# bs_w's weights loaded first and its first quarter made ahead of the one-hot rows; the last unit's gate and up products one unit further up

## What is computed

```python
# layer 0: one expert per sequence, the argmax of cond_8
expert = argmax(cond_8, -1)
up, gate = x @ W_up[expert].T + b_up, x @ W_gate[expert].T + b_gate
x = x + (silu(up) * gate) @ W_down[expert].T + b_down
# layer 1: a base matrix and a low-rank part, weighted by cond_8
x = x + x @ W_base.T + b_base + 2.0 * einsum('bter,eor,be->bto', einsum('btc,erc->bter', x, As), Bs, cond_8)
# layer 2: a weighted sum of eight masked matrices
x = x + einsum('bnt,bot->bno', x, einsum('bg,got->bot', cond_8, weight * mask)) + bias
# layer 3: the two best experts of each sequence and a shared one (gelu MLPs, 128 -> 512 -> 128)
x = x + sum over the 2 chosen of w * mlp(x, expert) + mlp(x, shared)
```

## Time and profile before

| | us |
|---|---|
| median of 3 runs | 153.5 (153.43 to 153.65) |
| the profiled execution | 153.69 |
| its span, first to last instruction | 151.7 |
| PE busy | 147.4 (97% of the span) |
| DVE, ACT, POOL busy | 109.8, 72.0, 91.4 |

### The profile page before, as it was taken

The page is one execution under the profiler, slowest core; times in us unless marked ns, Lnnn a source line. Parts: engine busy times, 40 slices in busy tenths (PEclk is TensorE's granted clock), DMA queues, the critical chain, the costliest instruction groups (busy, mean ns, idle before and its releaser), DMA issues.

```text
span 151.7 us, 3108 instructions
## 1 busy us (share of the span) xinstructions
PE 147.4 (97%) x1075; PEld 135.1 (89%) x1075; DVE 109.8 (72%) x229; ACT 72.0 (47%) x138; POOL 91.4 (60%) x93
## 2 busy tenths in 40 slices
PE   7999999999999999999999999999999999999992
PEld 2479999999978999999989999999999999999881
DVE  3985666667996586867775967876587895968772
ACT  2875444461375554454444354545425434345640
POOL 1003999999700007849994939995876999880000
PEclk9999999999999999999999999999999999999999
DMA  2999999974354676393397386095447047000052
GB/s 62 414 401 403 411 405 394 420 298 144 154 190 138 175 160 225 78 302 109 78 309 252 130 269 215 0 300 206 190 134 280 4 139 274 4 4 0 0 209 72
DMA packets 13912, 30.15 MB, mean 199 GB/s; under 512 B 1337, under 2 KB 8009, under 8 KB 13769
## 3 DMA queue, kind: packets, MB, share of 16 engines
q1 hardware_dynamic: 13472, 28.76, 54.7%
q10 hardware_dynamic: 424, 1.20, 2.0%
HBM read 24.71 MB, written 1.05 MB: 170 GB/s over the span
## 4 chain that ended last, share of the span: by engine, by line
PE 89%; DVE 4%; POOL 3%; ACT 2%; issue 1%; ACTq 0%; DVEq 0%; POOLq 0%
PE pair L550 22%; PE pair L540 12%; PE acc L599 10%; PE pair L482 10%; PE pair L557 8%; PE acc L584 6%; PE acc L608 5%; PE acc L490 5%; PE acc L438 2%; PE pair L526 2%; PE pair L497 2%; POOL duo_lo L372 2%; PE pair L471 2%; PE pair L445 2%; DVE hid L771 2%; ACT hid_hi L431 2%
## 5 line engine op out<-in xcount | busy, mean ns | idle before, releaser
L372 POOL TENSOR_TENSOR duo_lo<-raw_duo,duo_hi 128x512 fp32r<-128x512 f32 x36 | 48.6, 1350 | 2.9
L762 DVE TENSOR_TENSOR hid_lo<-hid,hid_hi 128x512 fp32r<-128x512 f32 (+1 forms) x41 | 36.1, 882 | 17.8 <-ACT hid_hi L431 17.3
L431 ACT ACTIVATE hid_hi<-hid 128x512 fp32r<-128x512 f32 (+1 forms) x41 | 25.4, 621 | 44.0 <-DVE hid L771 41.1
L369 POOL CAST duo_hi<-raw_duo 128x512 fp32r<-128x512 f32 x36 | 28.3, 786 | 28.5 <-PE acc L599 28.5
L771 DVE TENSOR_TENSOR hid<-pair,act 128x512 f32<-128x512 f32 (+1 forms) x49 | 32.9, 673 | 5.7 <-PE pair L550 4.2
L550 PE MATMUL pair<-x_duo,duo_hi 128*128 128x256 f32 x192 | 35.2, 281 | 0.2 <-POOL duo_lo L372 0.2
L412 ACT ACTIVATE act<-pair 128x512 f32<-128x512 f32 x48 | 28.3, 590 | 9.7 <-PE pair L550 7.7
L550 PEld LDWEIGHTS pair<-x_duo,duo_hi 128*128 128x128 f32 x192 | 29.7, 189 | 0.8 <-issue 0.3
L550 PE MATMUL pair<-x_duo,duo_lo 128*128 128x256 f32 x96 | 26.9, 280 | 0.0
L540 PE MATMUL pair<-x_hl,shared_hi 128*128 128x512 f32 x64 | 20.5, 401 | 0.1
L550 PEld LDWEIGHTS pair<-x_duo,duo_lo 128*128 128x128 f32 x96 | 18.0, 188 | 0.0
(11 more groups left out here) (101 smaller groups left out, 199.2 us busy)
## 6 DMA issues: line engine op xcount, KB each, us to landing
raw_duo<-experts SPq DMA_DIRECT2D x12, 768.0 KB, 5.2
ring<-experts SPq DMA_DIRECT2D x16, 386.5 KB, 6.7
raw_solo<-experts SPq DMA_DIRECT2D x8, 768.0 KB, 5.3
x_duo<-x_hl SPq DMA_DIRECT2D x24, 128.0 KB, 4.0
x<-xT ACTq DMA_DIRECT2D x1, 1024.0 KB, 6.2
lora_raw<-x SPq DMA_DIRECT2D x4, 256.0 KB, 2.4
raw_solo<-shared SPq DMA_DIRECT2D x1, 768.0 KB, 9.8
out<-lora_raw SPq DMA_DIRECT2D x3, 256.0 KB, 2.8
```

Source lines behind the costliest of these rows:

```text
L369: pool.tensor_copy(duo_hi[:, j % HALVES, piece(n)], raw_duo[:, j % RAWS, piece(n)])\
L372: pool.tensor_tensor(duo_lo[:, j % HALVES, piece(n)], raw_duo[:, j % RAWS, piece(n)], duo_hi[:, j % HALVES, piece(n)].bitcast(F32), ALU.su ...
L431: act.activation(hid_hi[:, k % SPLITS, at], hid3[:, u % PAIRS, at], ACT.Copy)\
L762: dve.tensor_tensor(hid_lo[:, k % SPLITS, at], hid3[:, u % PAIRS, at], hid_hi[:, k % SPLITS, at].bitcast(F32), ALU.subtract).then_inc(hid_ ...
```

## The change

SP issues `lora` ahead of `cond`. On DVE the loop body that makes a quarter of `bs_w` becomes `spread(q)`. `spread(0)` stands right behind `at_diag`, after waits for `cond_rep` and `lora`; then come the copy to `at_row`, `onehot`, `chosen_b` and the other three quarters. On PE the AT product is followed by `warm(2)` and `prepare1(0)`, then the rank products, then `prepare1(1)` to `prepare1(3)`; one of the three zero products behind the AT product is gone. In layer 3, `gateup(UNITS - 1)`, S15's, is issued right behind `gateup(UNITS - 2)`, so ahead of `down` of S12 and no longer behind it.

```diff
         @block.sync
         def _(sp):
+            sp.dma_start(lora_sb[:, :], lora).then_inc(lora_in, 16)
             sp.dma_start(cond_sb[:, :], cond).then_inc(cond_in, 16)
-            sp.dma_start(lora_sb[:, :], lora).then_inc(lora_in, 16)
             sp.dma_start(w2_sb[:, :, :], w2).then_inc(w2_in, 16)
...
             pe.matmul(acc[1][:, 0:B], ones_b[:, :], at_diag[:, :], start=True, stop=True).then_inc(at_mm, 1)
-            warm(1)
+            warm(2)
+            prepare1(0)
 
             pe.wait_ge(chosen_done, 1)
             pe.matmul(pair[2][0][0:B, 0:E], earlier_b[:, :], chosen_b[:, :], start=True, stop=True)
             pe.matmul(pair[2][0][0:B, E:2 * E], ones_b[:, 0:B], chosen_b[:, :], start=True, stop=True)\
               .then_inc(rank_mm, 1)
-            warm(2)
-            for q in range(G):
+            for q in range(1, G):
                 prepare1(q)
...
             for u in range(UNITS):
-                if u + AHEAD < UNITS:
+                if u + AHEAD < UNITS - 1:
                     gateup(u + AHEAD)
+                if u + AHEAD == UNITS - 2:
+
+                    gateup(UNITS - 1)
                 down(u)
...
-            step = [3]
...
-            dve.wait_ge(rep_in, 16)
-            dve.wait_ge(at_mm, 1)
-            dve.tensor_copy(at_row[:, :], acc[1][0:1, 0:B]).then_inc(at_done, 1)
-            dve.wait_ge(lora_in, 16)
-            for q in range(G):
+            def spread(q):
                 at = slice(q * GB, (q + 1) * GB)
...
                    .then_inc(bsw_done, 1)
+
+            dve.wait_ge(rep_in, 16)
+            dve.wait_ge(lora_in, 16)
+            spread(0)
+            dve.wait_ge(at_mm, 1)
+            dve.tensor_copy(at_row[:, :], acc[1][0:1, 0:B]).then_inc(at_done, 1)
+            step = [3]
...
+            for q in range(1, G):
+                spread(q)
```

More of the change, by code:

```diff
@@ L634, in _ @@
                .then_inc(at_diag_done, 1)
+            def spread(q):
+                at = slice(q * GB, (q + 1) * GB)
+                dve.scalar_tensor_tensor(
+                    bs_w[:, at, :], lora_sb[:, BS1:BS1 + P].unsqueeze(1).to_broadcast([P, GB, P]), LORA_SCALE,
+                    cond_rep[:, at].unsqueeze(2).to_broadcast([P, GB, P]), ALU.mult, ALU.mult)\
+                   .then_inc(bsw_done, 1)
+            dve.wait_ge(rep_in, 16)
[3 more added lines that the diff above has]
+            dve.tensor_copy(at_row[:, :], acc[1][0:1, 0:B]).then_inc(at_done, 1)
             step = [3]
```

## The result

The changed kernel took 156.69 us (median of 4 runs, 156.09 to 156.85) against 153.57 (153.43 to 154.0): a ratio of 1.0191, 95% interval 1.0157 to 1.0225. The forecast was 153.6 and the range ended at 154.1, so the time lies outside it. Measured a second time beside other runs of the kernel before (experiment 8), the ratio was 1.0116, interval 1.0068 to 1.0163. The ratios are not quotients of the medians printed. Two executions at a much lower mean clock, one of the kernel before (247.53 us, 0.57) and one of experiment 5 (694.33 us, 0.20), are left out of the ratios and spreads.

The account below looks back on a forecast made before the run. TensorE was taken as the bound, busy 147.4 of 151.7 us. Terms -0.43 + 0.60 - 0.04 = +0.13 put the profiled execution at 153.82 and the median at 153.6 us; range 153.2 to 154.1.

Parts of the forecast that it names:

- -0.43 + 0.60 - 0.04: Forecast sum in us: one zero product dropped, AT product later with cond, last product's wait in the tail gone; together +0.13.
- TensorE speeds up later: Rival: a gap ahead of the AT product delays TensorE's rise to full speed until 7.7 us; +1.4, 155.1 us; chance 0.10.
- d: Delay of cond's landing when issued second, passed to the AT product: 0.60 us, upper end 0.85, far low end 0.2.
- Part one: Opening transfers on SyncE: issuing lora ahead of cond makes cond land, and the AT product start, 0.60 us later.
- Part two: TensorE's opening list: one zero product less gives -0.43 us; rank products, 0.23, only move; prepare1(0) stays at 4.88.
- the covers behind it: Slack of steps moved later at the start: ring loads 1.4 us left, payload 0.5; claimed to cost nothing.
- Part three: Layer 3 tail: S15's gate and up products issued earlier remove TensorE's wait before the last product; -0.04 us, bounds -0.1 and +0.1.
- Slower: Outcome of the whole kernel slower by over 0.2% (0.31 us): chance 0.22, from 0.12 + 0.10.
- late cond: Rival: cond lands clearly behind lora, 0.85 us late; +0.38, 153.9 us; chance 0.12.
- late rise: The slower rival in which TensorE reaches full speed only at 7.7 us; +1.4; chance 0.10.
- the case that got 0.65: The forecast itself: cond delayed by 0.4 to 0.75 us, whole kernel +0.0 to +0.3; chance 0.65.
- The 0.31 us: About 0.2% of the whole kernel's time, claimed as what a measurement can tell from no change.

Follow-up runs that it names:

- experiment 8: The changed kernel measured again, nothing edited, beside many runs of the kernel before: 155.71 us against 154.15, ratio 1.0116.
- experiment 5: Kernel before with warm(3) for warm(5) ahead of the AT product, cond still first: 155.15 us against 154.15, ratio 1.0066.
- experiment 6: Kernel before with warm(4) for warm(5) ahead of the AT product: 155.52 us against 154.02, ratio 1.0084.
- experiment 1: Kernel before with only lora issued ahead of cond: 155.97 us against 153.94, ratio 1.0116.
- experiment 10: Kernel before with cond still first on SyncE but issued only after GpSimd's second memset, at 1.11 us: 156.58 us, one execution.
- experiment 12: Kernel before with cond first but issued late, and ScalarE issuing no transfer until cond has landed: 157.96 us, one execution.
- experiment 2: Changed kernel with warm(7) for warm(5), filling the break ahead of the AT product: 154.21 us against 153.94 for the kernel before, ratio 1.0021.
- experiment 3: Changed kernel with cond issued ahead of lora again: 154.24 us against 153.94 for the kernel before, ratio 1.0024.
- experiment 9: Kernel before with an unread second copy of cond (10 KB) issued ahead of cond on SyncE: 156.02 us against 154.15, ratio 1.013.
- experiment 11: Kernel before with lora ahead of cond, and cond_rep behind small and x on ScalarE's queue: 159.90 us, one execution.
- experiment 4: Kernel before with only S15's gate and up products moved one unit earlier in the tail: 154.09 us against 153.94, ratio 0.9994.

## Why the prediction was wrong

**The step that failed: the gap was given no term in the sum.** The sum is -0.43 + 0.60 - 0.04. It counts the late AT product, but takes TensorE's work behind the gap as running at the speed of before. The rival "TensorE speeds up later" named the mechanism and the place, and was given 0.10 because "the gap is 0.6 in 3.8". That argument is a proportion, and experiment 6 shows that the cost doesn't follow one: a break of 0.43 costs as much as one of 0.67, 1.0 to 1.5 us by the medians. So even with d at the 0.60 of the forecast the gap would have been there and would have cost more than 1 us. The term left out measured 2.35 in the first trace of the changed kernel (6.11 against the 3.76 that the new list takes at full speed, which is 3.85 - 0.09) and 0.98 in the second (4.74 against 3.76). The rival's price, +1.4, is of the right size. Its rise, "as long an unbroken stretch as before", 3.8 us from the AT product, was too early for the first trace (6.0 us, from 4.27 to about 10.2) and somewhat late for the second (3.2 us, from 4.25 to about 7.4).

**Part one, the order of the transfers: mis-sized, outside its bounds.** d was put at 0.60 with an upper end of 0.85; it was 0.95 and 0.93 in the two traces of the changed kernel and 1.84 in experiment 1. The upper end was taken from lora's own 2.4 us to landing. It looked for the delay in the queue that cond had been moved on, behind lora. As far as the single executions of experiments 10 and 12 show, it lay on the other one: issued 0.4 to 0.5 later, cond met the transfers of ScalarE (2.3 us with them, 1.7 without). The rule weighed there, from the Trainium skill's DMA: Bandwidth & Descriptors, that a semaphore's write follows the earlier writes of its DMA engine, gave a d of 0.70 by lora's landing. It is not contradicted, but lora is not what set the time: it was in by 0.75 + 2.2 = 2.95, cond at 3.42. Whether cond's end stood behind ScalarE's writes in this way, no run here separates.

**What happened, in one sum.** Start of layer 2's first product against the kernel before: in the first trace +0.95 (late data), -0.60 (one zero product less and the rank products moved), +0.33 (the rank products at their new place) and +2.35 (half speed), together 3.03. In the second +0.93, -0.60, +0.33 and +0.98, together 1.64. The spans differ by 2.9 and 1.6. So late data and new order cost 0.7, and the break the rest.

**Part two: right in its terms.** One zero product less gave -0.60 with the rank products moved out of that stretch (-0.43 - 0.23 was worked out). spread(0) was on time in the changed kernel (prepare1's first weights at 4.80, under the zero products); in experiments 2 and 3, with the rise ahead of prepare1(0), it came 0.1 too late for the weights to be loaded ahead. The rank products at their new place cost 0.33 and not 0.23. None of the covers behind it broke: payload was done at 12.73 and its product came three microseconds later, at 15.85, and TensorE never waited for a ring load. One reading was wrong and cost nothing: ScalarE's exponential did not follow cond, it started at 4.19 against 4.18 before, behind the load of its table.

**Part three: right.** -0.04 forecast, -0.03 in the trace: the product starts 0.61 behind hidden_low in all five traces with this part of the change, 0.63 to 0.65 in the others. By timing it is not to be told from zero.

**The chances.** Slower had 0.22, and its two cases, late cond and late rise, were added as if they excluded each other. They are one: a late cond is what opens the break, and the case that got 0.65 has a late cond too. With d at 0.95 alone the sum would have been +0.48; with the break it is outside the range. The 0.31 us that "a measurement of this kernel can tell from no change" was too fine as well: with ten runs against 25 the intervals still reach 0.4 us to either side and more.

No version tried here beats the kernel before.

## What to carry to other kernels

Zero products that keep TensorE going can decide when TensorE reaches its full speed even when nothing reads them: after an edit that delays the first real product, look first at whether the fill still reaches it, and put the missing ones in before judging the edit. The first small transfer that everything hangs on should be issued before any other engine's transfers, as far as experiments 9 to 12 go, and its latency in one place tells little about its latency half a microsecond later. Two effects with one trigger are one case with the sum of their prices.

## What the hardware showed that was not expected

The half speed of TensorE's start doesn't appear in the granted clock, which reads 1.00 in every stretch up to 12 us in both traces; it can only be read from the spacing of matmuls (0.86 against 1.71 us for a prepare1 product). The moment of the rise was 4.8 and 6.9 us in two traces of the same opening list, and 7.4 against 10.2 in two of the changed one. Without a break it came 2.9 to 5.9 us behind the first zero product (four traces: the kernel before, experiments 2, 3 and 4). With one it came 3.0 to 6.0 us behind the first product after the break (seven traces: the changed kernel twice, experiments 1, 5, 6, 9 and 10), about the same spread. Within it the length of the break, from 0.43 to 1.84 us, shows no order. The Trainium skill's TensorE: Matmul & The Clock Gate, Part 1, says that the watching of TensorE's activity runs free and doesn't begin with the kernel, so that the point of the rise differs from run to run; the differing agrees with these traces, its reason they don't show. In the series of the experiments the runs of the kernel before spread over 1.35 to 1.64 us, where the first four had spread over 0.6: a difference of 0.3% can't be judged from three or four runs of this kernel.

A break of 0.43 us in the opening work cost 1.3 to 1.5 us (interval of the ratio 0.55 to 1.12%). A transfer of 10 KB took 1.5 to 1.7 us when issued at 0.75, and 2.2 to 3.2 when issued at 1.1 to 1.2, with ScalarE's transfers issued in the meantime; in the one execution without them it took 1.7 there too.
